# A decoder layer with routed experts: two products for the last 64 inner rows, the lower outputs added on VectorE, each tile's expert read ahead of the transposes

## The chip, the cores and the metric

The kernel runs on one core of one Trainium2 chip. The metric is the device time of an execution in microseconds. The kernel before took 1031.85 us (median of 3 runs, 1031.57 to 1033.68).

## The reference, cut to what matters

The layer is a state-space mixer, a cross attention and a routed feed-forward block, each added to x (2048 tokens of 256 numbers, fp32). The change lies in the last block:

```python
scores = xt @ Wg.T                                   # 2048 tokens, 8 experts
topk_scores, topk_idx = jax.lax.top_k(scores, 2)
gate = jax.nn.silu(jnp.einsum('td,ehd->teh', xt, W1))  # H = 704 inner rows
up = jnp.einsum('td,ehd->teh', xt, W2)
y = jnp.einsum('teh,edh->ted', gate * up, W3)
...
out = jnp.einsum('te,ted->td', w, y)                 # w: the two scores of a token
```

## The kernel before

Two phases follow each other: `mixer_phase` (everything up to the router's scores, to about 700 us) and `routed_ffn_phase`, the only one that the diff touches.

**Sorting.** VectorE and TensorE work out for each token its two positions in a list sorted by expert. Each expert's rows are padded to whole tiles of 128, so there are at most NT = 39 tiles, and all 39 are computed. With these inputs the list ends before the last ones. The table `tile_expert` holds each tile's expert. GpSimd gathers the 39 tiles of tokens (`tok`), and SP copies tile i + 4 to `tok_in` after it has stored the output of tile i (`store_and_load`).

**One tile.** TensorE transposes 128 tokens (ps_x). ScalarE rounds them to fp32r (`tokT_hi`) and VectorE keeps the rest (`tokT_lo`), and the weights are split in the same way (`w_hi`, `w_lo`). A product is then made as three: hi by hi, hi by lo, lo by hi. `gate_up` makes the gate and up products, 24 matmuls of 352 columns in two halves c = 0 and 1. ScalarE applies SiLU (`act_`) and VectorE multiplies by up (`multiply`, into `hid`). `transpose_hidden` transposes the 704 inner values in six pieces, five of 128 rows and the last of 64 (H_LAST). ScalarE (`round_hidden`) and VectorE (`rest_of_hidden`) split them. `down` makes 6 x 3 matmuls of 256 columns into ps_y, `evacuate` copies that to `y_sb`, and SP stores it to `ffn_sorted` in HBM.

**Order on TensorE.** The work is skewed by one tile: for tile i it is transpose_hidden(i-1), transpose_tokens(i+1), gate_up(i), down(i-1). Two tiles make one `pair`, which a hardware loop (`Fori`, L1581) repeats, and the last tiles are written out. `expert(i)` is a register load from `tile_expert` by PE's own sequencer (L1514); gate_up and down each make one, right ahead of their matmuls.

**Weights.** An expert's weights lie in one of two buffers. SP loads experts 0 to 3 and GpSimd experts 4 to 7 (`load_expert`, `reload`), with four DMAs each. The last, L1129, brings the 64 remaining rows of W3. The lower 64 partitions of that piece, in the weights and in hidT, are zero from a memset and two casts at the phase's start (`w_pad`), so all matmuls run over 128 rows. GpSimd splits the weights of experts 2 to 7, each as soon as the tiles of the expert two before are done (`next_expert`, `split`).

**The end.** Each token has a lower and an upper position. GpSimd gathers the lower outputs (`fetch` into `y_one`) when the tiles of experts 0 to 6 are stored (`stored(0)`). It waits for all sixteen, multiplies and adds the first eight groups of tokens into `x_all` (L1258, L1261), and then gathers the upper outputs (`y_two`, the space of `tok`) once all used tiles are stored (`stored(1)`). VectorE adds the other eight lower groups ahead of the last evacuation (L1481), combines all sixteen with the upper ones (L1491), and SP stores two groups at a time.

Of the kernel before, what the change touches and what calls it, by code (L numbers as in the profile page):

```python
# [5 lines left out]
F32 = mybir.dt.float32  # L6
# [14 lines left out]
def at(i, n=1):  # L21
    return bass.ds(i, n)
# [989 lines left out]
def routed_ffn_phase(nc, io, dims, env, sem, buf):  # L1012
# [12 lines left out]
    LOOP = NT + 2  # L1025

    with ExitStack() as ctx:
# [12 lines left out]
        hid = sb("hid", [P, 2, HF])  # L1040
# [62 lines left out]
        w_pad, hi_ok, w_ok = sem("w_pad"), sem("hi_ok"), sem("w_ok")  # L1103
# [14 lines left out]
        low_part, low_in, low_in2 = sem("low_part"), sem("low_in"), sem("low_in2")  # L1118
        BY_POOL = G // 2

        def load_expert(eng, e, p, done):

            w, full, last = w_raw[:, p, :], (KH - 1) * P, NW - D
            for n, src in enumerate((io["w1T"], io["w2T"])):
# [4 lines left out]
            eng.dma_start(w[0:H_LAST, last:NW], io["w3T"][at(e), full:HF, :].rearrange("a p d -> p (a d)")  # L1129
                          ).then_inc(done, 16)  # L1130
# [10 lines left out]
        with nc.Block() as block:  # L1141
# [42 lines left out]
            def _(pool):  # L1184
# [47 lines left out]
                for p in range(2):  # L1232
                    next_expert(2 + p, p, first_ld[p], 128)
                    reload(pool, 2 + p, p, wts_ld[p])
                with pool.Fori(2, E // 2 - 1) as j:
                    for p in range(2):
                        next_expert(2 * j + p, p, wts_ld[p], 64 * (j - 1))
                        reload(pool, 2 * j + p, p, wts_ld[p])
                for p in range(2):
                    next_expert(E - 2 + p, p, wts_ld[p], 64 * (E // 2 - 2))  # L1240
# [25 lines left out]
            def _(act):  # L1266
# [11 lines left out]
                def round_hidden(i):  # L1278
# [3 lines left out]
                    nc.scalar.copy(hidT_hi[:, 4:KH - 1, :], ps_h1[:, 0:(KH - 5) * P].rearrange("p (c m) -> p c m", m=P)  # L1282
                                   ).then_inc(hT_hi, 1)
                    nc.scalar.copy(hidT_hi[0:H_LAST, KH - 1, :], ps_h1[0:H_LAST, (KH - 5) * P:(KH - 4) * P]).then_inc(hT_hi, 1)

                act.wait_ge(w_pad, 1)
                for p in range(2):

                    act.wait_ge(first_ld[p], 64)
# [25 lines left out]
            def _(dve):  # L1315
# [118 lines left out]
                def rest_of_hidden(i):  # L1434
                    for k, (c, n, rows_in, bank) in enumerate(((0, 4, P, ps_h0), (4, KH - 5, P, ps_h1), (KH - 1, 1, H_LAST, ps_h1))):
                        dve.wait_ge(hT_hi, 3 * i + (1 if k == 0 else 3))
                        wait(dve, y_mm, i)
                        col = c % 4 * P if k < 2 else (KH - 5) * P
                        nc.vector.tensor_tensor(hidT_lo[0:rows_in, c:c + n, :],  # L1439
                                                bank[0:rows_in, col:col + n * P].rearrange("p (c m) -> p c m", m=P),  # L1440
                                                hidT_hi[0:rows_in, c:c + n, :].bitcast(F32), ALU.subtract).then_inc(hT_lo, 1)
# [25 lines left out]

                pair(1)
# [3 lines left out]
                rest_of_tokens(NT - 1, 0)  # L1472
                multiply(NT - 2, 1)
                evacuate(NT - 3, 0)
                rest_of_hidden(NT - 2)
                multiply(NT - 1, 0)
                evacuate(NT - 2, 1)
                rest_of_hidden(NT - 1)
                dve.wait_ge(low_ld, 16 * G)
                for g in range(BY_POOL, G):  # L1480
                    nc.vector.scalar_tensor_tensor(out=x_all[:, g, :], in0=y_one[:, g, :], scalar=w_low[:, 0, g:g + 1],  # L1481
                                                   in1=x_all[:, g, :], op0=ALU.mult, op1=ALU.add).then_inc(low_in2, 1)
                evacuate(NT - 1, 0)

                for g in range(G):
                    if g < BY_POOL:
                        dve.wait_ge(low_in, g + 1)
                    else:
                        dve.wait_ge(low_in2, g - BY_POOL + 1)
# [5 lines left out]
            def _(pe):  # L1495
# [33 lines left out]
                def gate_up(i, p):  # L1529
                    e = expert(i)  # L1530
# [13 lines left out]
                def transpose_hidden(i, p):  # L1544
# [5 lines left out]
                    for c in range(4, KH):  # L1550
                        n = P if c < KH - 1 else H_LAST
                        last = nc.tensor.transpose(ps_h1[0:n, (c - 4) * P:(c - 3) * P], hid[:, p, c * P:c * P + n], ident[:])  # L1552
                    last.then_inc(h_mm, 1)

                def down(i):
# [5 lines left out]
                    for c in range(KH):  # L1561
                        for n, (x, w) in enumerate(parts):
# [80 lines left out]
```

## Time and profile before

| | |
|---|---|
| median of 3 runs | 1031.85 us |
| profiled execution | 1034.26 us |
| its span, first to last instruction | 1032.4 us |
| mean granted TensorE clock | 0.916 |
| TensorE busy | 883.8 us (86%), 5148 matmuls |
| VectorE busy | 669.6 us (65%) |
| ScalarE busy | 447.0 us (43%) |
| GpSimd busy | 606.3 us (59%) |

Engines are PE (TensorE's matmuls), PEld (its weight loads), DVE (VectorE), ACT (ScalarE), POOL (GpSimd) and SP; a q behind the name is the engine's sequencer or DMA queue. L1563 is line 1563 of the kernel before. Times of instructions count from the span's start. Matmuls overlap in the array, so their starts tell more than their durations. In the chain of waits, "issue" is time in which an engine waited for nothing that the profile shows.

### The profile page before, as it was taken

How to read it: one execution, taken by the hardware profiler on the slowest of the kernel's cores; microseconds unless marked ns; L12 is line 12 of the kernel's file. 1: busy time of each engine (PE TensorE's matmuls, PEld its weight loads, DVE VectorE, ACT ScalarE, POOL GpSimd, SP SyncE). 2: the span in 40 equal slices, each digit the busy share in tenths (PEclk: the TensorE clock that was granted, in tenths of full speed). 3: DMA queues.
4: the chain of work that ended last, by engine and by line, in shares of the span. 5: the costliest groups of instructions: out<-in, count | busy, mean ns of one | idle time of the engine just before them, and what ended most of it. 6: DMA issues, size and time to landing. Idle time of an engine off the chain costs nothing. (4 is left out here: it accounts for less than half of the span.)

```text
span 1032.4 us, 16281 instructions
## 1 busy us (share of the span) xinstructions
PE 883.8 (86%) x5148; PEld 709.2 (69%) x5149; DVE 669.6 (65%) x1091; ACT 447.0 (43%) x827; POOL 606.3 (59%) x499
## 2 busy tenths in 40 slices
PE   5766776999998999988999778973699999999991
PEld 2334354667776676876588655763599999999991
DVE  4089789888799888798788943327643443444344
ACT  2544755446764547664456512223122333233230
POOL 2056787487766487766887613200778663355575
PEclk9979876999996999998999968995799999999996
DMA  9560013000044000063000400004464513311324
GB/s 313 185 234 1 0 43 122 2 16 1 2 183 145 1 17 1 2 220 107 9 10 1 140 25 16 1 21 168 155 215 105 172 45 115 120 41 36 101 66 154
DMA packets 48955, 85.45 MB, mean 83 GB/s; under 512 B 6292, under 2 KB 38696, under 8 KB 46856
## 3 DMA queue, kind: packets, MB, share of 16 engines
q1 hardware_dynamic: 43032, 65.77, 18.9%
q0 software_dynamic: 5872, 19.02, 6.2%
q8 instruction: 29, 0.48, 0.2%
q14 instruction: 22, 0.18, 0.1%
HBM read 65.64 MB, written 14.55 MB: 78 GB/s over the span
## 5 line engine op out<-in xcount | busy, mean ns | idle before, releaser
L417 POOL TENSOR_TENSOR u<-dtx,b_all 128x512 f32<-128x512 f32 x256 | 326.1, 1287 | 148.2 <-DVE h L666 140.8
L666 DVE TENSOR_TENSOR_SCAN h<-da,u 128x512 f32<-128x512 f32 x256 | 307.5, 1215 | 44.3 <-ACT da L501 27.1
L501 ACT ACTIVATE da<-dt_,a_neg 128x512 f32<-128x512 f32 x256 | 175.3, 691 | 119.5 <-DVE h L666 118.6
L789 PEld LDWEIGHTS ysum<-ident,h 128*128 128x128 f32 x1024 | 129.1, 152 | 68.3 <-issue 36.2
L789 PE MATMUL ysum<-ident,h 128*128 128x128 f32 x1024 | 150.2, 290 | 16.0 <-DVE h L666 11.1
L969 PE MATMUL pv<-pT,ctx_n 128*128 128x128 f32 (+1 forms) x832 | 103.6, 276 | 2.0 <-ACT pT L568 1.7
L969 PEld LDWEIGHTS pv<-pT,ctx_n 128*128 128x128 f32 (+1 forms) x832 | 98.1, 192 | 6.4 <-ACT pT L568 2.1
L940 PE MATMUL pa<-ctx_t,xnT_a 128*128 128x401 f32 (+1 forms) x256 | 93.7, 502 | 3.4 <-DVE sim L649 2.0
L1425 DVE TENSOR_TENSOR hid<-act_,ps_u 128x352 f32<-128x352 f32 x78 | 40.7, 521 | 84.0 <-ACT act_ L1276 84.0
L778 PE MATMUL pm<-xs,w_dt 128*128 128x512 f32 x128 | 71.5, 667 | 10.9 <-ACT sp_pos L537 4.7
L1276 ACT ACTIVATE act_<-ps_g 128x352 f32<-128x352 f32 x78 | 36.3, 465 | 102.2 <-PE ps_u L1539 102.2
L772 PE MATMUL pm<-xnT_m,w_in 128*128 128x512 f32 x128 | 68.7, 654 | 7.9 <-DVE xs L623 5.2
L940 PEld LDWEIGHTS pa<-ctx_t,xnT_a 128*128 128x128 f32 x256 | 45.3, 190 | 33.6 <-DVE sim L649 5.2
L1563 PE MATMUL ps_y<-w_hi,hidT_hi 128*128 x234 | 66.2, 283 | 2.1 <-DVE hidT_lo L1439 2.0
L1563 PE MATMUL ps_y<-w_hi,hidT_lo 128*128 x234 | 66.3, 283 | 0.0
L1563 PE MATMUL ps_y<-w_lo,hidT_hi 128*128 x234 | 66.1, 283 | 0.0
L1228 POOL DMA_INDIRECT tok<-xn_dram,tok_id x39 | 43.9, 1127 | 35.8 <-DVE tok_id L1407 24.2
L1281 ACT CAST hidT_hi<-ps_h 128x512 fp32r<-128x512 f32 x39 | 22.9, 587 | 90.9 <-PE ps_h L1552 90.9
L649 DVE COPY_PREDICATED sim<-mask,pa 128x401 f32<-128x401 uint8 x64 | 38.4, 601 | 34.8 <-PE pa L940 22.3
L1439 DVE TENSOR_TENSOR hidT_lo<-ps_h,hidT_hi 128x512 fp32r<-128x512 f32 (+2 forms) x117 | 42.0, 415 | 28.4 <-ACT hidT_hi L1281 28.4
L1202 POOL TENSOR_TENSOR w_lo<-w_raw,w_hi 128x2816 fp32r<-128x2816 f32 (+1 forms) x12 | 58.6, 4883 | 0.0
L440 POOL TENSOR_SCALAR sim<-mask,neg_c 128x1601 f32<-128x1601 uint8 x16 | 25.7, 1605 | 54.9 <-PE pa L955 27.5
(217 smaller groups left out, 1739.2 us busy)
## 6 DMA issues: line engine op xcount, KB each, us to landing
b_all<-b_dram SPq DMA_DIRECT2D x16, 1024.0 KB, 4.9
ctx_t<-in_ctxT SPq DMA_DIRECT2D x4, 1601.0 KB
ctx_n<-in_ctx SPq DMA_DIRECT2D x4, 1536.0 KB
ffn_sorted<-yg SPq DMA_DIRECT2D x1, 4992.0 KB, 22.5
ffn_sorted<-y_sb SPq DMA_DIRECT2D x39, 128.0 KB, 1.7
tok_in<-tok SPq DMA_DIRECT2D x35, 128.0 KB, 2.0
mask<-in_mask SPq DMA_DIRECT2D x16, 200.1 KB, 2.4
w_raw<-in_w1T SPq DMA_DIRECT2D x4, 704.0 KB, 4.4
```

The costliest lines, as they stand in the source:

```text
L417: nc.gpsimd.tensor_tensor(u[:, i % 2, :], dtx[:, j % 2, :], b_all[:, n, :], ALU.mult).then_inc(u_ok, 1)
L501: nc.scalar.activation(da[i % DS][:], dt_[:, j % 2, :], ACT.Exp, scale=a_neg[:, j, n:n + 1]).then_inc(da_ok, 1)
L666: nc.vector.tensor_tensor_scan(h[:, i % HS, :], da[i % DS][:], u[:, i % 2, :], 0.0, ALU.mult, ALU.add).then_inc(scan_ok, 1)
L772: last = nc.tensor.matmul(bank[:], w_in[:, k, j * P:(j + 1) * P], xnT_m[:, k, :], start=k == 0, stop=k == KD - 1)
L778: last = nc.tensor.matmul(DT_BANKS[j][:], w_dt[:, k, j * P:(j + 1) * P], of_row(xs, b, k), start=k == 0, stop=k == KI - 1)
L789: last = nc.tensor.matmul(ysum[:, t * P:(t + 1) * P], h[:, i % HS, t * P:(t + 1) * P], ident[:], is_transpose=True, start=n == 0 and t == ...
L940: last = nc.tensor.matmul(pa[c % 2][:, 0:hi - lo], xnT_a[:, k, q * P:(q + 1) * P], ctx_t[:, k, lo:hi], start=k == 0, stop=k == KD - 1)
L969: last = nc.tensor.matmul(pv[:, k * P:(k + 1) * P], ctx_n[0:w, c, k * P:(k + 1) * P], pT[0:w, c, :], start=c == 0 and k == 0, stop=c == KC ...
L1202: nc.gpsimd.tensor_tensor(w_lo[:, p * NW + lo:p * NW + hi], w_raw[:, p, lo:hi], w_hi[:, p * NW + lo:p * NW + hi].bitcast(F32), ALU.subtrac ...
L1228: pool.indirect_dma_start(tok[:, i, :], None, xn3_dram, bass.IndirectOffsetOnAxis(ap=tok_id[:, i:i + 1], axis=0)).then_inc(tok_ld[i // 2 % ...
L1439: nc.vector.tensor_tensor(hidT_lo[0:rows_in, c:c + n, :], bank[0:rows_in, col:col + n * P].rearrange("p (c m) -> p c m", m=P), hidT_hi[0:r ...
L1563: last = nc.tensor.matmul(ps_y[:, 0:D], x[:, c, :], w[:, at(e % 2 * NW + (2 * NGU + c * D), D)], start=c == 0 and n == 0, stop=c == KH - 1 ...
```

## The change

1. **Two products for the last piece.** `hid` is 768 columns wide. For c = 1, VectorE first writes the last 64 columns once more behind the 704. The sixth transpose then has 128 rows: the last 64 inner rows twice. ScalarE rounds all of it in one cast with the piece ahead of it (two casts in place of three), and VectorE replaces the lower copy by its remainder, in place: the piece holds hi on top and lo below. The last 64 rows of W3 are loaded twice, into both halves, by one more DMA per expert. `down` needs two products for this piece, by w_hi and by w_lo, so it has 17 matmuls. The memset and the casts of zeros are gone, and each expert counts five DMAs (WLD = 80).
2. **Lower outputs.** GpSimd no longer multiplies and adds: it goes from the gather of y_one to `stored(1)` and the gather of y_two. VectorE adds all sixteen lower groups (`add_lower`) in five lots of 3, 3, 3, 4 and 3, between its work for tiles 36 to 38.
3. **Expert.** In `pair` and in the last tiles, `expert(i)` for gate_up is read ahead of the transposes instead of behind them.

```diff
+    WLD = 16 * 5
-        hid = sb("hid", [P, 2, HF])
+        hid = sb("hid", [P, 2, KH * P])
...
             eng.dma_start(w[:, 2 * NGU:last].rearrange("p (c d) -> p c d", d=D), ...
-            eng.dma_start(w[0:H_LAST, last:NW], io["w3T"][at(e), full:HF, :].rearrange("a p d -> p (a d)")
-                          ).then_inc(done, 16)
+            for half in range(2):
+                eng.dma_start(w[half * H_LAST:(half + 1) * H_LAST, last:NW],
+                              io["w3T"][at(e), full:HF, :].rearrange("a p d -> p (a d)")).then_inc(done, 16)
...
                 stored(0)
                 fetch(y_one, 0, lambda g: low_ld)
-                pool.wait_ge(low_ld, 16 * G)
-                for g in range(BY_POOL):
-                    nc.gpsimd.tensor_scalar(y_one[:, g, :], y_one[:, g, :], w_low[:, 0, g:g + 1], None,
-                                            ALU.mult).then_inc(low_part, 1)
-                    pool.wait_ge(low_part, g + 1)
-                    nc.gpsimd.tensor_tensor(x_all[:, g, :], x_all[:, g, :], y_one[:, g, :], ALU.add).then_inc(low_in, 1)
                 stored(1)
                 fetch(y_two, 1, lambda g: up_ld[g // 2])
...
-                    nc.scalar.copy(hidT_hi[:, 4:KH - 1, :], ps_h1[:, 0:(KH - 5) * P].rearrange("p (c m) -> p c m", m=P)
+                    nc.scalar.copy(hidT_hi[:, 4:KH, :], ps_h1[:, 0:(KH - 4) * P].rearrange("p (c m) -> p c m", m=P)
                                    ).then_inc(hT_hi, 1)
-                    nc.scalar.copy(hidT_hi[0:H_LAST, KH - 1, :], ps_h1[0:H_LAST, (KH - 5) * P:(KH - 4) * P]).then_inc(hT_hi, 1)
-
-                act.wait_ge(w_pad, 1)
...
-                nc.vector.memset(w_raw[H_LAST:P, :, NW - D:NW], 0.0).then_inc(w_pad, 1)
-                dve.wait_ge(w_pad, 1)
-                for part in (hidT_hi, hidT_lo):
-                    nc.vector.tensor_copy(part[H_LAST:P, KH - 1, :], w_raw[H_LAST:P, 0, NW - D:NW - D + P]).then_inc(w_pad, 1)
...
+                        if c == 1:
+                            nc.vector.tensor_tensor(hid[:, p, HF:KH * P], act_[:, HF - H_LAST:HF],
+                                                    ps_u[c][:, HH - H_LAST:HH], ALU.mult)
                         nc.vector.tensor_tensor(hid[:, p, c * HH:(c + 1) * HH], ...
...
+                    low_half = hidT_hi[H_LAST:P, KH - 1, :]
+                    nc.vector.tensor_tensor(low_half, ps_h1[H_LAST:P, (KH - 5) * P:(KH - 4) * P], low_half.bitcast(F32),
+                                            ALU.subtract).then_inc(hT_lo, 1)
...
+                def add_lower(first, last):
+
+                    dve.wait_ge(low_ld, 16 * G)
+                    for g in range(first, last):
+                        nc.vector.scalar_tensor_tensor(out=x_all[:, g, :], in0=y_one[:, g, :], scalar=w_low[:, 0, g:g + 1],
+                                                       in1=x_all[:, g, :], op0=ALU.mult, op1=ALU.add).then_inc(low_in, 1)
...
                 rest_of_tokens(NT - 1, 0)
+                add_lower(0, 3)
                 multiply(NT - 2, 1)
                 evacuate(NT - 3, 0)
+                add_lower(3, 6)
                 rest_of_hidden(NT - 2)
+                add_lower(6, 9)
                 multiply(NT - 1, 0)
                 evacuate(NT - 2, 1)
+                add_lower(9, 13)
                 rest_of_hidden(NT - 1)
-                dve.wait_ge(low_ld, 16 * G)
-                for g in range(BY_POOL, G):
-                    nc.vector.scalar_tensor_tensor(...)
+                add_lower(13, G)
                 evacuate(NT - 1, 0)
...
                     for c in range(KH):
-                        for n, (x, w) in enumerate(parts):
+                        for n, (x, w) in enumerate(parts if c < KH - 1 else parts[0:2]):
...
                 def pair(i):
                     for k in range(2):
+                        e = expert(i + k)
                         transpose_hidden(i + k - 1, k)
                         transpose_tokens(i + k + 1, k)
-                        gate_up(i + k, 1 - k)
+                        gate_up(i + k, 1 - k, e)
                         down(i + k - 1)
```

## Rows read from the trace of the kernel before

**Rows 1.** busy time by stage: TensorE, its weight loads, VectorE, ScalarE, GpSimd, clock, DMA
```profile
720.00:740.00 20.00, 11.37 (x49) 10.13 (x49) 11.54 (x23) 1.79 (x5) 12.13 (x9) 0.58 0.38 127
780.00:820.00 40.00, 40.00 (x290) 39.85 (x290) 16.83 (x41) 12.11 (x36) 35.45 (x25) 1.00 0.46 135
```

**Rows 2.** chain of waits in order of time, one tile (start us, us, what)
```profile
834.93 0.96 PE ps_g L1539 x6
...
838.77 2.15 PE ps_y L1563 x18
841.79 1.03 PE ps_g L1539 x6
```

**Rows 3.** chain of waits, start-up, one stall, and the last gather
```profile
700.20 0.50 DVE w_raw L1331
...
741.65 0.60 issue
...
750.10 7.27 DMA tok_in<-tok
...
757.92 0.80 issue
758.72 1.22 PE ps_g L1539 x6
...
890.24 0.83 issue
...
1024.09 2.89 DMA tok<-ffn_sorted,pos
```

**Rows 4.** timeline of TensorE, first matmuls of tiles 31, 35, 38 and last down
```profile
953.32 0.42 PE L1539 MATMUL ps_g<-w_hi,tokT_hi 128*128 x1
...
981.06 0.42 PE L1539 MATMUL ps_g<-w_hi,tokT_hi 128*128 x1
...
1001.42 0.41 PE L1539 MATMUL ps_g<-w_hi,tokT_hi 128*128 x1
...
1010.36 0.38 PE L1563 MATMUL ps_y<-w_hi,hidT_hi 128*128 x1 [2.04 <-DVE hidT_lo L1439]
```

**Rows 5.** timeline of GpSimd, the two gathers and the work between
```profile
963.53 1.03 POOL L1243 DMA_INDIRECT y_one<-ffn_sorted,pos  x1 [0.52 <-issue]
...
982.40 0.95 POOL L1243 DMA_INDIRECT y_one<-ffn_sorted,pos  x1 [0.30 <-issue]
985.24 0.93 POOL L1258 TENSOR_SCALAR y_one<-y_one,w_low 128x256 f32<-128x256 f32 x1 [1.90 <-DMA y_one<-ffn_sorted,pos]
...
1000.69 1.03 POOL L1243 DMA_INDIRECT tok<-ffn_sorted,pos  x1 [0.54 <-issue]
...
1010.79 3.24 POOL L1243 DMA_INDIRECT tok<-ffn_sorted,pos  x1 [0.30 <-issue]
```

**Rows 6.** timeline of VectorE, one tile's product, and the end
```profile
839.30 0.52 DVE L1425 TENSOR_TENSOR hid<-act_,ps_u 128x352 f32<-128x352 f32 x1 [1.38 <-ACT act_ L1276]
...
1009.97 3.23 DVE L1481 SCALAR_TENSOR_TENSOR x_all<-y_one,w_low,x_all 128x256 f32<-128x256 f32 x8
...
1013.47 3.23 DVE L1491 SCALAR_TENSOR_TENSOR x_all<-tok,w_low,x_all 128x256 f32<-128x256 f32 x8
...
1027.07 0.88 DVE L1491 SCALAR_TENSOR_TENSOR x_all<-tok,w_low,x_all 128x256 f32<-128x256 f32 x2 [1.53 <-DMA tok<-ffn_sorted,pos]
```

**Rows 7.** PE's sequencer by line, ns and start, behind the loop's branch of tile 15
```profile
L1581 PEldq FUSED_REGOPS  x1: 59/59/59, 839.5 to 839.5; - x1
...
L1514 PEldq TENSOR_LOAD <-tile_expert x1: 300/300/300, 840.5 to 840.5; - x1
...
L1539 PEldq FUSED_REGOPS  x1: 104/104/104, 841.4 to 841.4; - x1
```

**Rows 8.** timeline of all engines where an expert's reload begins
```profile
883.45 0.76 POOL L1125 DMA_DIRECT2D w_raw<-in_w1T  x1 [0.30 <-POOL w_lo L1202]
...
883.66 0.49 SPq L1152 DMA_DIRECT2D tok_in<-tok  x1
```

More of the change, by code:

```diff
@@ L1232, in _ @@
                 for p in range(2):
-                    next_expert(2 + p, p, first_ld[p], 128)
+                    next_expert(2 + p, p, first_ld[p], 2 * WLD)
                     reload(pool, 2 + p, p, wts_ld[p])
@@ L1434, in rest_of_hidden @@
                 def rest_of_hidden(i):
[L1435 to L1441, printed above, removed]
+                    wait(dve, y_mm, i)
+                    dve.wait_ge(hT_hi, 2 * i + 1)
+                    for c, n, bank in ((0, 4, ps_h0), (4, KH - 5, ps_h1)):
+                        if c:
+                            dve.wait_ge(hT_hi, 2 * i + 2)
+                        nc.vector.tensor_tensor(hidT_lo[:, c:c + n, :], bank[:, 0:n * P].rearrange("p (c m) -> p c m", m=P),
+                                                hidT_hi[:, c:c + n, :].bitcast(F32), ALU.subtract).then_inc(hT_lo, 1)
+                    low_half = hidT_hi[H_LAST:P, KH - 1, :]
+                    nc.vector.tensor_tensor(low_half, ps_h1[H_LAST:P, (KH - 5) * P:(KH - 4) * P], low_half.bitcast(F32),
+                                            ALU.subtract).then_inc(hT_lo, 1)
                 def evacuate(i, p):
@@ L1472, in _ @@
                 rest_of_tokens(NT - 1, 0)
+                add_lower(0, 3)
                 multiply(NT - 2, 1)
                 evacuate(NT - 3, 0)
+                add_lower(3, 6)
                 rest_of_hidden(NT - 2)
+                add_lower(6, 9)
                 multiply(NT - 1, 0)
                 evacuate(NT - 2, 1)
+                add_lower(9, 13)
                 rest_of_hidden(NT - 1)
-                dve.wait_ge(low_ld, 16 * G)
-                for g in range(BY_POOL, G):
-                    nc.vector.scalar_tensor_tensor(out=x_all[:, g, :], in0=y_one[:, g, :], scalar=w_low[:, 0, g:g + 1],
-                                                   in1=x_all[:, g, :], op0=ALU.mult, op1=ALU.add).then_inc(low_in2, 1)
+                add_lower(13, G)
                 evacuate(NT - 1, 0)
                 for g in range(G):
[L1486 to L1489, printed above, removed]
+                    dve.wait_ge(low_in, g + 1)
                     dve.wait_ge(up_ld[g // 2], 32)
@@ L1527, in transpose_tokens, with gate_up @@
                     last.then_inc(x_mm, 1)
-                def gate_up(i, p):
-                    e = expert(i)
+                def gate_up(i, p, e):
                     pe.wait_ge(w_ok, 2 * e + 1)
@@ L1550, in transpose_hidden @@
                     for c in range(4, KH):
-                        n = P if c < KH - 1 else H_LAST
-                        last = nc.tensor.transpose(ps_h1[0:n, (c - 4) * P:(c - 3) * P], hid[:, p, c * P:c * P + n], ident[:])
+                        last = nc.tensor.transpose(ps_h1[:, (c - 4) * P:(c - 3) * P], hid[:, p, c * P:(c + 1) * P], ident[:])
                     last.then_inc(h_mm, 1)
@@ L1561, in down @@
                     for c in range(KH):
-                        for n, (x, w) in enumerate(parts):
+                        for n, (x, w) in enumerate(parts if c < KH - 1 else parts[0:2]):
                             last = nc.tensor.matmul(ps_y[:, 0:D], x[:, c, :],
                                                     w[:, at(e % 2 * NW + (2 * NGU + c * D), D)],
-                                                    start=c == 0 and n == 0, stop=c == KH - 1 and n == 2)
+                                                    start=c == 0 and n == 0, stop=c == KH - 1 and n == 1)
                     last.then_inc(y_mm, 1)
-                pe.wait_ge(w_pad, 3)
                 transpose_tokens(0, 0)
                 transpose_tokens(1, 1)
-                gate_up(0, 0)
+                gate_up(0, 0, expert(0))
                 def pair(i):
                     for k in range(2):
+                        e = expert(i + k)
                         transpose_hidden(i + k - 1, k)
                         transpose_tokens(i + k + 1, k)
-                        gate_up(i + k, 1 - k)
+                        gate_up(i + k, 1 - k, e)
                         down(i + k - 1)
@@ L1584, in _ @@
                 transpose_tokens(NT - 1, 0)
-                gate_up(NT - 2, 1)
+                gate_up(NT - 2, 1, expert(NT - 2))
                 down(NT - 3)
                 transpose_hidden(NT - 2, 1)
-                gate_up(NT - 1, 0)
+                gate_up(NT - 1, 0, expert(NT - 1))
                 down(NT - 2)
```

11 lines of the change are left out of this document (5 added, 6 removed).

## The prediction

> **What bounds the kernel now.** I read the table by stage first. From 780 to 820 us the matrix unit is busy 40.00 of 40 us at a granted clock of 1.00 [rows 1]: while the experts' tiles run, TensorE is the bound. The chain of waits gives one tile: its gate and up products start at 834.93, the 18 down products take 2.15 us, and the next tile starts at 841.79, 6.86 us later [rows 2]. One down product is therefore 2.15 / 18 = 0.12 us. Tile 3 starts at 758.72 [rows 3] and tile 38, the last, at 1001.42 [rows 4]: 242.70 us for 35 tiles, which is 2.6 us more than 35 x 6.86. Part of the 2.6 us is one stall of 0.83 us at 890.24 [rows 3]; the rest is small ones.
>
> After the tiles the bound changes. The chain that ended last doesn't leave through TensorE: it goes through GpSimd's queue [rows 5]. The first gather (y_one) starts at 963.53, the eight multiply-and-add pairs at 985.24, and the second gather (y_two) only at 1000.69. Its last issue is at 1024.09 and lands 2.89 us later [rows 3]; VectorE combines from 1027.07 for 0.88 us [rows 6], and the span ends at 1032.4, that is 4.45 us after the last combination. The last tile's first down product is at 1010.36 [rows 4], long before. So the tail is GpSimd's order of work: what brings the second gather forward is gained until VectorE takes over.
>
> When may the second gather start? It waits for the last used tile. The reference's inputs route 354, 538, 550, 585, 609, 596, 366 and 498 rows to the experts, which fill 3, 5, 5, 5, 5, 5, 3 and 4 tiles, 35 in all; tiles 35 to 38 are computed but never gathered. The first gather waits for tile 30, the second for tile 34.
>
> **The down products.** 39 tiles lose one product of 0.12 us each. The array-bound tile goes from 6.86 to 6.74 us. That only comes through if nothing else ends last. The hidden transposes wait for VectorE's product (0.52 us from 839.30 [rows 6]), then PE's sequencer issues eight transposes, loads the tile's expert at 840.5 and reaches the gate products at 841.4 [rows 7], while the array runs dry at about 841.5. On tiles behind the loop's branch (tile 15, 841.79) the sequencer is the later of the two by 0.07 us, which the chain shows as 1.03 instead of 0.96 for the first six products [rows 2]. With the shorter down and the load left in place, those tiles would gain nothing.
>
> **The expert's load moved ahead.** From the load to the gate products is 0.9 us, at most 0.75 of it the load's own [rows 7]. Ahead of the transposes it lies in the wait for the hidden product. Behind the branch (over at 839.6) the sequencer has 0.2 us until that product is there at 839.8, so transposes would be issued at 840.35 instead of 839.9. The array needs them at 840.92 less 0.12 [rows 2]: hidden, with some 0.4 us to spare. Bounds: nothing, or the whole 0.75 on 18 tiles if the array needed them sooner. I take hidden. Where the array stood idle the load is plainly on the path: 0.60 us at 741.65 and 0.80 at 757.92 [rows 3]. At 741.65 the next down product waits for VectorE's weight split, so I count nothing; at 757.92 I count 0.75.
>
> **Duplicated columns and rows.** VectorE's extra product covers 64 of the 352 columns that cost 0.52 [rows 6]; between 0.09 (in proportion) and 0.52, taken as 0.2. It delays the transposes' release, which has 0.8 us to spare before the array arrives. ScalarE's two casts in place of three, and VectorE's third subtraction on the upper 64 rows, are off the path. The second copy of the last 64 rows is one more DMA per expert, 64 KB, on SP for experts 0 to 3 and on GpSimd for 4 to 7. GpSimd has over 15 us between experts. On SP it lies ahead of the load of tile 4, which took 7.27 us behind weights [rows 3]. 64 KB more there is 0.1 to 0.6 us; I take 0.35. The memset at the start (0.50 us [rows 3]) and two casts of some 0.2 us go from VectorE's chain; it still needs GpSimd's counters, so I take 0.6 of the 0.9 (bounds 0 and 0.9).
>
> **Token loads against weight loads.** The 0.83 at 890.24 follows a token load that SP issued at 883.66, 0.21 us behind GpSimd's first weight load at 883.45 [rows 8]. GpSimd's split of an expert has a fixed length, two tiles get 0.24 us shorter or more, so the token load slips ahead of the weights. I count 0.5 us of stalls kept instead of 1.3.
>
> **The sum up to the last tile.** Tile 3: 0.6 (start) + 0.12 (down of tile 0) + 0.75 (expert) - 0.35 (DMA) = 1.1 us earlier. Tiles 3 to 38: 35 x 6.74 + 0.5 = 236.4 instead of 242.7, 6.3 less. Tile 38 starts at 994.0.
>
> **The tail.** Tile 31's start to the first gather, across tile 30's down and its store, is 963.53 - 953.32 = 10.21 us [rows 4, 5]. Tile 35 started at 981.06; it starts 1.1 + 5.8 = 6.9 earlier, so the second gather could start at 974.15 + 10.21 - 0.12 = 984.2. GpSimd is free by then, its pairs, which held it from 985.24 on, being gone and its first gather being over at about 977. That is 16.5 us earlier than 1000.69. Fifteen issues of the first gather took 982.40 - 963.53 = 18.87 us to the start of the sixteenth, 1.26 each [rows 5]; undisturbed, the last issue of the second starts at 1003.1 and ends at 1004.0.
>
> They are disturbed. The issue at 1010.79 took 3.24 us instead of 0.95, and ended at 1014.03, 0.83 after VectorE's eight additions (1009.97 + 3.23) [rows 5, 6]: an issue that starts while VectorE adds SBUF to SBUF waits for the run's end. The new kernel has five such runs, of 3, 3, 3, 4 and 3 additions at 0.404 us. Each holds up at most one issue, by 0 to 1.65 us; I take half, 2.9 in all. The last issue then starts near 1006.0 and ends at 1006.9, landing 1.9 us later.
>
> VectorE: y of tile 37 is copied out at about 1000.2, 0.4 us long, and four additions of 0.404 us follow; the subtraction on tile 38's hidden values, possible from 1001.3, comes behind them, 0.95 us late. Tile 38's down products start at 1010.36 - 7.4 - 0.12 + 0.95 = 1003.8, and the sixteen combinations at 1006.7, by the 3.1 us between the two before [rows 4, 6] less a product and a small overlap. They take 16 x 0.404 = 6.46 us and end at 1013.15, with all of y_two landed. Plus 4.45, plus 0.3 for eight output stores close together: a span of 1017.9, 14.5 less. The profiled execution took 1034.26 us, 1.86 more than its span, and the median of the runs is 1031.85; the difference goes to the median: 1017.3 us.
>
> The Trainium skill ("SBUF — State Buffer", two separate sides) calls the port pair of VectorE and GpSimd a lock held for a whole instruction, and lets a VectorE operation with two SBUF inputs take it only against a GpSimd operation that reads SBUF. By that condition an issue that only writes its descriptors would not be held up, and the last would end at 1004.0: the sum stays, since VectorE ends last in it, and the first rival below falls away. The row of 3.24 us speaks against it.
>
> **Rivals.** *The last gather is held up by the combinations* (0.24). If the five runs cost over 3.6 us instead of 2.9, GpSimd's last issue starts after 1006.7, when VectorE starts fourteen combinations in a row. These end at 1012.4, the issue 0.83 later, it lands after another 1.9, and two combinations end at 1016.0, 2.9 later than in the sum: 1020.2 us. For it: the two times lie within 0.7 us. Against it: runs of three end before most issues have waited long.
> *The tiles gain less* (0.13). Token loads behind the weights' extra 64 KB wait at each reload, or the sequencer still ends last behind the branch. The tiles then give 3 us instead of 6.3: 1020.6 us.
> *The stalls vanish altogether* (0.08): start and tiles give 1.5 more, 1015.8.
> *The change doesn't do what it says*: the pairs leave GpSimd, but the second gather is as late as before (0.02). That needs tile 37 or 38 among the used ones, which the rows per expert exclude. The gain would be the 7 us of the tiles: 1025.
> *Slower* (0.04): the granted clock. It was 0.58 from 720 to 740 and 1.00 afterwards [rows 1]; a tile at half clock costs 6.7 us more. If a moved wait near tile 4 let it fall, the sum turns from 14.5 / 6.7 = 2.2 such tiles on; with four, 1044. Of the chance, 0.01 is for about two such tiles and no change. Against it: that wait gets shorter, and before it stood at 1.00 through it.
>
> **How the numbers follow.** The forecast has 0.49, the rivals 0.24, 0.13, 0.08, 0.02 and 0.04. A measurement of this kernel tells 0.2% (2 us) from no change. Faster 0.96, within 0.2% 0.01, slower 0.03. The unknown terms (start 0 to 0.9, extra DMA 0.1 to 0.6, stalls 0 to 1.3, held-up issues 0 to 6.5) and the first three rivals give 1014.5 to 1022.5.
>
> **What would show it.** Right: 17 down products per tile, starts 6.74 apart on both kinds of tile; no issue time behind the token transposes near 757; the second gather's first issue near 984; VectorE's combinations as one run from 1006.7. Wrong: a steady tile above 6.8, idle TensorE ahead of the hidden transposes on every second tile, GpSimd issues of over 2 us between 990 and 1005, or a last issue that ends after a run of fourteen combinations.

## The result, and the profile after

The changed kernel takes 1018.16 us (median of 5 runs, 1017.06 to 1019.81) against 1033.60 for the kernel before (median of 5, the three of the prediction among them): a ratio of 0.9855 (95% interval 0.9833 to 0.9877). A later set of both gave 0.9829 (0.9787 to 0.9872). 1017.3 was forecast. The profiled execution took 1017.61 us, its span is 1015.8, its mean granted clock 0.921.

The total is right, but its last 0.9 us is luck: the span came out 2.1 us under the sum and the step from the span to the median 3.0 us over it. Two terms of the sum are wrong: held-up gather issues that don't occur, and an end that comes sooner than I added. The chain of waits shows start-up, one stall and one tile.

```profile
732.80 2.12 PE ps_g L1538 x6
...
749.22 8.18 DMA tok_in<-tok
...
757.53 0.43 PE ps_x L1526 x2
758.01 1.22 PE ps_g L1538 x6
...
799.06 6.35 DMA tok_in<-tok
...
806.04 1.22 PE ps_g L1538 x6
...
813.04 0.96 PE ps_g L1538 x6
...
816.86 2.04 PE ps_y L1561 x17
...
819.77 0.32 PE ps_g L1538 x2
```

Against [rows 2]: 17 down products in 2.04 us instead of 18 in 2.15, and the next gate products 6.73 us behind the last. 6.73 to 6.76 is the distance of all tiles from 4 to 37 but one, whether they follow the loop's branch or not; tile 38, ahead of which no tokens are left to transpose, comes 6.52 us behind tile 37 (6.64 before). Against [rows 3]: the issue time between the token transposes and tile 3's gate products (0.80) is gone, but the load ahead of it took 8.18 us instead of 7.27. A second late load (799.06) makes the one stall left: tile 10 starts 7.59 us behind tile 9.

The end, first TensorE (timeline, the first gate product and the first down product of tile 38), then GpSimd, then VectorE.

```profile
994.53 0.41 PE L1538 MATMUL ps_g<-w_hi,tokT_hi 128*128 x1
...
1004.13 0.38 PE L1561 MATMUL ps_y<-w_hi,hidT_hi 128*128 x1 [2.83 <-DVE hidT_hi L1435]
```
```profile
976.53 0.95 POOL L1244 DMA_INDIRECT y_one<-ffn_sorted,pos  x1 [0.30 <-issue]
983.01 0.20 POOL L1211 TENSOR_TENSOR pool_scrap<-ident 128x1 f32<-128x1 f32 x1 [5.52 <-DMA ffn_sorted<-y_sb]
...
984.35 0.98 POOL L1244 DMA_INDIRECT tok<-ffn_sorted,pos  x1 [0.52 <-issue]
...
1002.06 1.06 POOL L1244 DMA_INDIRECT tok<-ffn_sorted,pos  x1 [0.31 <-issue]
1003.43 0.95 POOL L1244 DMA_INDIRECT tok<-ffn_sorted,pos  x1 [0.30 <-issue]
```
```profile
1001.03 1.66 DVE L1467 SCALAR_TENSOR_TENSOR x_all<-y_one,w_low,x_all 128x256 f32<-128x256 f32 x4
1002.61 0.88 DVE L1432 TENSOR_TENSOR hidT_lo<-ps_h,hidT_hi 128x512 fp32r<-128x512 f32 x2
...
1003.85 1.28 DVE L1467 SCALAR_TENSOR_TENSOR x_all<-y_one,w_low,x_all 128x256 f32<-128x256 f32 x3
1006.46 0.42 DVE L1441 COPY y_sb<-ps_y 128x256 f32<-128x256 f32 x1 [1.34 <-PE ps_y L1561]
1006.80 6.41 DVE L1491 SCALAR_TENSOR_TENSOR x_all<-tok,w_low,x_all 128x256 f32<-128x256 f32 x16
```

GpSimd is idle 5.52 us until tile 34 is stored, and the second gather begins at 984.35, not at 1000.69 [rows 5]. Its sixteen issues are 1.27 us apart on the mean; the last ends at 1004.38, 2.4 us before VectorE is ready to combine. The sixteen combinations run through from 1006.80 to 1013.21, and the span ends 2.6 us later.

What ends the span can be read on the line that closes the program: each engine has a DRAIN there, and the program is over when the last of them is. First the kernel before, then the changed one (ns, and start in us):

```profile
L1141 POOLq DRAIN  x1: 24336/24336/24336, 1007.9 to 1007.9; - x1
...
L1141 SPq DRAIN  x1: 7/7/7, 1030.3 to 1030.3; - x1
```
```profile
L1142 POOLq DRAIN  x1: 19997/19997/19997, 991.9 to 991.9; - x1
...
L1142 SPq DRAIN  x1: 7/7/7, 1015.6 to 1015.6; - x1
```

In the kernel before, SP, which waits for the output stores, is done at 1030.3 and GpSimd only at 1007.9 + 24.3 = 1032.2: GpSimd ends the span. In the changed kernel GpSimd is done at 1011.9 and SP at 1015.6: the output stores end it.

The 16.6 us between the two spans divide so. Tile 0 starts at 732.80 instead of 733.90: 1.1. Tiles 0 to 3 take 25.21 instead of 24.82: -0.4. Tiles 3 to 38 take 236.52 instead of 242.70: 6.2. From tile 38's start to the end, 21.3 instead of 31.0: 9.7. These are distances in one profile of each kernel, and the start-up and the stalls differ from profile to profile by some 2 us.

### The profile page after: what moved, and what is told of

The parts are those of the page before. It is cut to its first block and busy times, and to the rows that moved or that the text cites. A ratio compares the mean times of both kernels' runs of the same rounds, so it can differ in the third digit from the quotient of the medians.

```text
span 1015.8 us, 16089 instructions
## 1 busy us (share of the span) xinstructions
PE 876.1 (86%) x5109; PEld 703.4 (69%) x5110; DVE 684.3 (67%) x1135; ACT 445.5 (44%) x788; POOL 592.2 (58%) x487
## 5 line engine op out<-in xcount | busy, mean ns | idle before, releaser
L1229 POOL DMA_INDIRECT tok<-xn_dram,tok_id x39 | 44.6, 1143 | 35.3 <-DVE tok_id L1396 23.7
L1561 PE MATMUL ps_y<-w_hi,hidT_lo 128*128 x195 | 55.3, 284 | 0.0
L1538 PE MATMUL ps_g<-w_hi,tokT_hi 128*128 x156 | 53.8, 345 | 0.7 <-issue 0.6
L1432 DVE TENSOR_TENSOR hidT_lo<-ps_h,hidT_hi 128x512 fp32r<-128x512 f32 x78 | 34.6, 486 | 28.3 <-ACT hidT_hi L1276 28.3
```

The lines of the kernel that those rows point to most:

```text
L1229: pool.indirect_dma_start(tok[:, i, :], None, xn3_dram, bass.IndirectOffsetOnAxis(ap=tok_id[:, i:i + 1], axis=0)).then_inc(tok_ld[i // 2 % ...
L1538: last = nc.tensor.matmul(out[:, 0:HH], x[:, p, k * P:(k + 1) * P], w[:, at(e % 2 * NW + (first + k * HF), HH)], start=k == 0 and n == 0, ...
L1561: last = nc.tensor.matmul(ps_y[:, 0:D], x[:, c, :], w[:, at(e % 2 * NW + (2 * NGU + c * D), D)], start=c == 0 and n == 0, stop=c == KH - 1 ...
```

## Experiments

Ratios are to the kernel before on the same chip. Distances are between first gate products (the first matmul of each tile); "35 tiles" is tile 3 to tile 38. A lot is one call of `add_lower`.

**The third product put back** for the last piece, all else changed.

```diff
-  for n, (x, w) in enumerate(parts if c < KH - 1 else parts[0:2]):
+  for n, (x, w) in enumerate(parts if c < KH - 1 else parts[0:2] + parts[0:1]):
```


> The changed kernel with a third matmul for the last piece again (the first of its two products is made once more, so the last 64 inner rows count too much in the output). If the array bounds the tiles, as forecast, each of 35 steady tiles goes from 6.74 back to 6.86 us, and the span from 1015.8 to about 1020.3 (39 x 0.12). Rival: something beside the array ends last in a tile (sequencer, VectorE), then the product is free: tiles stay at 6.74 and the span within 0.5 of 1015.8.

Measured: 1022.16 us, 0.9894 (0.9866 to 0.9922). The tile is 6.86 us again, with 2.15 us for x18 in the chain of waits:

```profile
864.74 2.15 PE ps_y L1561 x18
...
867.77 0.96 PE ps_g L1538 x6
```
35 tiles take 239.93 us, which is 34 x 6.86 and 6.64 for tile 38, without a stall. So the product is worth its 0.12 us on each tile, 4.0 us in the medians. The stall at tile 10 is absent. It goes with the time at which the token load that it waits for is issued, counted from the first of GpSimd's weight loads: 2.35 us behind it in the changed kernel's second profile (stall 1.9), 3.8 in its first (0.85), 4.15 in the kernel before with the expert ahead (0.2), 4.6 here and 5.0 in the kernel before (none). A longer tile puts the load further behind the weight loads.

**The expert read behind the transposes**, as before.

```diff
-                        e = expert(i + k)
                         transpose_hidden(i + k - 1, k)
                         transpose_tokens(i + k + 1, k)
+                        e = expert(i + k)
```


> The changed kernel with each tile's expert read behind the transposes, as before; all else stays. Forecast theory: the sequencer is released by VectorE's product, which now ends 0.14 us later, and then needs transposes, load and gate products in a row: the tiles behind the loop's branch take about 7.0 us and the others about 6.9 instead of 6.74, the span is 5 to 8 us longer (1021 to 1024). Rival 1: only the tiles behind the branch lose, 0.1 to 0.2 us each: 2 to 3 us. Rival 2: the load is hidden wherever it stands: under 0.5 us.

Measured: 1027.10 us, 0.9942 (0.9920 to 0.9964); 35 tiles take 244.33 us, more than the 242.70 of the kernel before. The tiles alternate between 7.06 and 6.89. The chain of waits, a tile behind the branch and the one after it, and VectorE in one of them:

```profile
909.54 0.44 PE ps_h L1547 x4
...
910.42 0.06 issue
910.48 1.22 PE ps_g L1538 x6
...
914.56 2.04 PE ps_y L1561 x17
...
917.47 1.12 PE ps_g L1538 x6
```
```profile
901.15 0.22 DVE L1415 TENSOR_TENSOR hid<-act_,ps_u 128x64 f32<-128x64 f32 x1 [1.30 <-ACT act_ L1271]
901.29 0.51 DVE L1417 TENSOR_TENSOR hid<-act_,ps_u 128x352 f32<-128x352 f32 x1
```
The first group of gate products takes 1.22 or 1.12 us where it needs 0.96: the array has run dry and waits for its sequencer. This is a loop that doesn't pass through the down products: gate and up products, SiLU, VectorE's product, the transposes' release, the expert's load, the next gate products. VectorE's new 64-column product sits in it and puts off the 352-column one by 0.14 us (901.15 to 901.29).

The starts of matmuls on TensorE's timeline show the loop's two parts. Here it is tiles 23, 24 and 25:

```profile
896.53 0.42 PE L1538 MATMUL ps_g<-w_hi,tokT_hi 128*128 x1
...
903.42 0.42 PE L1538 MATMUL ps_g<-w_hi,tokT_hi 128*128 x1
...
910.48 0.42 PE L1538 MATMUL ps_g<-w_hi,tokT_hi 128*128 x1
```
From a tile's first gate product to the end of VectorE's 352-column product (901.29 + 0.51) it is 5.27 us, against 5.13 in the kernel before (834.69 to 839.82): 0.14 more. From there to the next tile's first gate product it is 1.62 us, and 1.78 or 1.79 when that tile is behind the branch (1.78 in the kernel before, 839.82 to 841.60). The sums, 6.89 and 7.06, are the two distances; so the sequencer's part is fixed, and VectorE's 0.14 us goes into every tile. Without the 64-column product the same parts would give 6.91 behind the branch and 6.75 elsewhere; that is worked out, no run has it. I had forecast no gain for the tiles behind the branch with the load left in place; they lose 0.1 us, and the other tiles gain nothing. In the medians the load's place is worth 8.9 us.

**The expert ahead alone**, in the kernel before.

```diff
+                        e = expert(i + k)
                         transpose_hidden(i + k - 1, k)
                         transpose_tokens(i + k + 1, k)
-                        gate_up(i + k, 1 - k)
+                        gate_up(i + k, 1 - k, e)
...
```


> The kernel before with nothing changed but each tile's expert read ahead of the transposes. Forecast theory: tiles behind the loop's branch lose their 0.05 to 0.1 us of waiting for the sequencer, so all steady tiles take 6.86 to 6.87, and the idle 0.80 us near 757.9 goes: tile 3 starts 0.7 earlier and the tiles take 1 us less, but the end is GpSimd's, whose first gather moves by 1.5: the span gets 0.7 to 2 us shorter. Rival: behind the branch the load now ends last and those tiles get longer (over 6.96), the span is the same or longer.

Measured: 1029.98 us, 0.9979 (0.9961 to 0.9998). All tiles are 6.86 us (one stall, 7.08), 35 of them 240.13, which is 2.6 less than in the kernel before, where 1 was expected. 1.1 of the 2.6 is the kernel before's stall ahead of tile 22 (7.96), which its second profile doesn't have there; the other 1.5 is the up to 0.1 us by which most tiles lay above 6.86. So by itself the move is worth about 1.5 us of the tiles; together with the shorter down it decides whether that one counts at all.

**GpSimd's eight pairs put back**, VectorE's eight additions in one lot.

```diff
                 fetch(y_one, 0, lambda g: low_ld)
+                pool.wait_ge(low_ld, 16 * G)
+                for g in range(BY_POOL):
+                    nc.gpsimd.tensor_scalar(y_one[:, g, :], ...)
+                    nc.gpsimd.tensor_tensor(x_all[:, g, :], ...)
                 stored(1)
...
-                add_lower(0, 3) ... add_lower(9, 13)
-                add_lower(13, G)
+                add_lower(BY_POOL, G)
```


> The changed kernel with GpSimd's eight multiply-and-add pairs between the gathers again and VectorE's other eight additions in one lot ahead of the last evacuation. Forecast theory: the second gather starts at about 994.5 instead of 984.35, its last issue ends between 1014.4 and 1017, and the span is 1021 to 1024. Rival: the end is VectorE's anyway, because its combinations can't start before 1006; then the span stays below 1018.

Measured: 1024.61 us, 0.9926 (0.9901 to 0.9952). The second gather starts at 992.88; from tile 38 to the end it is 28.1 us instead of 21.3, so the pairs are worth 6.8 us (6.5 in the medians). Its last issue ends at 1013.4, GpSimd's DRAIN at 1020.9 and SP's at 1019.4, the span at 1021.1: it is GpSimd's end again. GpSimd's timeline beside VectorE's:

```profile
992.88 1.04 POOL L1245 DMA_INDIRECT tok<-ffn_sorted,pos  x1 [0.54 <-issue]
...
1004.25 1.23 POOL L1245 DMA_INDIRECT tok<-ffn_sorted,pos  x1 [0.30 <-issue]
...
1008.27 1.21 POOL L1245 DMA_INDIRECT tok<-ffn_sorted,pos  x1 [0.30 <-issue]
```
```profile
1001.79 3.26 DVE L1474 SCALAR_TENSOR_TENSOR x_all<-y_one,w_low,x_all 128x256 f32<-128x256 f32 x8
...
1005.42 4.04 DVE L1497 SCALAR_TENSOR_TENSOR x_all<-tok,w_low,x_all 128x256 f32<-128x256 f32 x10
```
Five issues start within these two runs, and the longest is 1.23 us. An issue that meets such a run is not always held up.

**No second copy of the last rows** for experts 2 to 7.

```diff
-            for half in range(2):
+            for half in range(halves):      # halves = 1 for experts 2 to 7
```


> The changed kernel without the second copy of the last 64 rows of W3 for experts 2 to 7 (the upper half keeps the rows of expert 0 or 1, so the output is another). If that DMA is what makes the token load of tile 4 land 0.9 us later (8.18 instead of 7.27) and the one of tile 12 stall TensorE for 0.85 us, both get shorter: tile 3 starts 0.5 to 0.9 earlier, the stall is below 0.5, the span 1 to 1.7 shorter (1014.1 to 1014.8). Rival: the stall comes from when the token load is issued relative to the weights, not from 64 KB more; then it stays within 0.2 us.

Measured: 1016.09 us, 0.9833 (0.9804 to 0.9861). Tile 3 starts 8.73 us behind tile 2 (9.37 in the changed kernel, 7.83 in its second profile, below), and the stall at tile 10 (the expectations count it as tile 12) is 7.63, as in the changed kernel. The 64 KB don't make the stall; their cost at tile 3 is lost in what that load varies by between profiles, and the interval of the ratio overlaps those of the changed kernel (0.9855 and 0.9829).

**All sixteen additions in one lot**, behind the last hidden remainder; and **two lots of eight**.

```diff
-                add_lower(0, 3) ... add_lower(9, 13)
+                add_lower(0, G)      # one lot: in place of add_lower(13, G)
+                add_lower(0, 8) ... add_lower(8, G)      # two: ahead of both rest_of_hidden
```


> The changed kernel with all sixteen lower additions in one lot between the subtraction on tile 38's hidden values and the last evacuation. The lot runs from about 1002.7 for 6.4 us, so the evacuation and the combinations start some 2.7 us later (1009.5). Theory of the forecast (an issue that starts during a run of VectorE additions waits for the run's end): the two or three gather issues that are left then wait up to 5 us, the last ends near 1012 and lands at 1014: span 1019 to 1022. Rival (only operations or runs of a certain kind hold it up, as no issue was held up in the changed kernel): issues stay at 0.96 us and the span is 1018 to 1019, set by VectorE's order alone.

> The changed kernel with the lower additions in two lots of eight (3.2 us each), behind the evacuation of tile 36 and of tile 37. Theory that long runs hold up GpSimd's gather issues: one issue in each lot takes 2 to 3.3 us instead of 0.96, and the last ends 2 to 5 us later (1006.5 to 1009.5 instead of 1004.4). Rival: all issues stay at 0.96 us, because what held up the two issues before lay elsewhere. Both: tile 38's down products come 1.5 to 3 us later than 1004.1, since the lots delay tile 37's and tile 38's subtractions, and the span is 1017 to 1020.

Measured: 1019.92 us, 0.9881 (0.9846 to 0.9916), and 1019.61, 0.9874 (0.9838 to 0.9909). In one lot only the last gather issue was left; it began 0.02 us ahead of the additions and took 0.95 us, so this run hardly tests the theory. The additions lie on the path ahead of the last evacuation, and the combinations start at 1009.07. In two lots, the last issue inside each took 1.22 and 1.25 us and the last of all ended at 1003.67, so the theory fails here. The second lot holds back tile 38's remainders, and then something else comes up (chain of waits):

```profile
1000.84 0.23 PE ps_h L1547 x2
...
1002.36 1.67 DVE x_all L1467 x4
...
1005.47 4.00 PE ps_y L1558 x17
```
The seventeen down products, which need 2.3 us, take 4.00. The table by stage shows the granted clock as 0.50 there (1.2 of 2.4 GHz), behind 4.4 us in which TensorE did nothing and within which it had begun to fall (0.90):

```profile
1001.07:1005.47 4.40, 0.00 (x0) 0.01 (x1) 4.05 (x11) 0.86 (x2) 2.21 (x2) 0.90 0.42 120
1005.47:1007.87 2.40, 2.40 (x11) 2.40 (x12) 0.00 (x0) 0.00 (x0) 0.00 (x0) 0.50 0.00 0
```

**Tiles 4 and 5 transposed straight from the token tile**, to take away the load ahead of tile 3; and again, with the changed kernel, on one chip.

```diff
+        DIRECT = 6
-                    load(i + AHEAD, (q + AHEAD) % GROUP)
+                    if not (isinstance(i, int) and i + AHEAD < DIRECT):
+                        load(i + AHEAD, (q + AHEAD) % GROUP)
...
-                    if isinstance(i, int) and i < AHEAD:
+                    if isinstance(i, int) and i < DIRECT:
```


> The changed kernel with one more pair of tiles written out on TensorE, and tiles 4 and 5 transposed straight from the gathered tokens, so that no copy of them queues behind the weights of expert 3. Theory: the 1.5 us for which tile 3 waits for that copy go, tile 5 starts 1 to 1.6 us earlier and so does all that follows, span 1014.3 to 1015.0. Rival: the wait turns up again at the first tile that is copied (tile 6), or a later copy meets weights that come as early as before, and the span stays within 0.5 us of 1015.8.

> The changed kernel, unchanged, beside the one with tiles 4 and 5 transposed straight from the tokens, on one chip: 1018 us within 1.5, the wait ahead of tile 3 (9.4 us between the first gate products of tiles 2 and 3, where a steady tile has 6.74) and one stall near tile 12 (7.6 us) again. No gather issue longer than 1.3 us from 984 us on, if the held-up issues don't belong to this kernel; one or more of 2 us and over if it is chance.

> Tiles 4 and 5 transposed straight from the token tile, as before, timed beside the changed kernel on one chip. If the wait ahead of tile 3 is really removed, the time is 1.0 to 2.6 us less than the changed kernel's (9.37 less 6.74 at most); if it only moves to the next loads, which then wait in the same queue, less than 1 us. From tile 0 to tile 38 the trace should then need 1 to 2.6 us less, or the same.

Measured: 1015.90 us (0.9852, 0.9821 to 0.9883) at first; on one chip 1016.76 (0.9831, 0.9788 to 0.9873) beside 1016.96 for the changed kernel: no difference. In the second profile the wait at tile 3 is gone (6.73), but tile 8 now starts 7.66 behind tile 7, and tile 10 8.42 behind tile 9. Its chain of waits:

```profile
782.72 6.22 POOL w_lo L1207
...
789.22 1.22 PE ps_g L1542 x6
...
796.31 7.48 DMA tok_in<-tok
```
From tile 0 to tile 38 it needs 260.9 us and the changed kernel's second profile 261.3. Without the wait at tile 3 the tiles reach the next expert's weights sooner and wait for their split (6.22) and for the token load behind their DMAs. The wait is moved, not removed. In the changed kernel's second profile the distances of tiles 3 and 10 were 7.83 and 8.65 where the first had 9.37 and 7.59: 16.5 and 17.0 in sum. No gather issue in it took over 1.1 us.

**The kernel before, profiled a second time.** 

> The kernel before, unchanged, profiled a second time: do GpSimd's two held-up gather issues (3.24 and 3.19 us, in the profile of before) come again? If VectorE's run of eight 128x256 additions holds an issue up as a matter of course, both come back at about 3.2 us. If it is a matter of when in the run the issue starts, or of chance, they take 0.95 to 1.25 us as in the changed kernels, and the last issue ends some 2 to 4 us sooner after the run before it. In both cases the steady tile is 6.86 us, and the time is within 2.5 us of 1033 us.

Measured: 1033.22 us. GpSimd and VectorE:

```profile
1010.19 0.95 POOL L1243 DMA_INDIRECT tok<-ffn_sorted,pos  x1 [0.30 <-issue]
1011.45 3.20 POOL L1243 DMA_INDIRECT tok<-ffn_sorted,pos  x1 [0.30 <-issue]
1014.95 0.95 POOL L1243 DMA_INDIRECT tok<-ffn_sorted,pos  x1 [0.30 <-issue]
```
```profile
1010.58 3.24 DVE L1481 SCALAR_TENSOR_TENSOR x_all<-y_one,w_low,x_all 128x256 f32<-128x256 f32 x8
...
1014.87 4.10 DVE L1491 SCALAR_TENSOR_TENSOR x_all<-tok,w_low,x_all 128x256 f32<-128x256 f32 x10
```
The first held-up issue comes again (it ends at 1014.65, 0.83 us after the run), the second doesn't, though it meets a longer run. The kernel with the expert ahead alone had both (3.02 and 3.19). 35 tiles took 245.12 us here, against 242.70: its stalls (the longest distance is 9.29, ahead of tile 12) differ between its two profiles by more than the changed kernel's.

**One gather more, after the eighth combination**, in the changed kernel.

```diff
+                sp.wait_ge(low_ld, 16 * (G + 1))
                 sp.wait_ge(out_st, 16 * (G // 2))
...
                 fetch(y_two, 1, lambda g: up_ld[g // 2])
+                pool.wait_ge(comb, 8)
+                pool.indirect_dma_start(y_one[:, 0, :], None, ffn_sorted, ...pos[:, 0, 0:1]...).then_inc(low_ld, 16)
```


> The changed kernel with one gather more (into y_one's first group, which is no longer read), issued by GpSimd after VectorE's eighth combination. In three profiles of kernels that have the old tail (the kernel before, its second look, and the one with the expert ahead only) the span ends 8.3 to 8.4 us after the start of GpSimd's last gather issue, although the last combination is over 4 to 5 us earlier; in the changed kernel it ends 12.4 us after it and 2.6 us after the last combination. Theory: GpSimd's part of the program ends a fixed 8.3 us after its last gather issue, whatever else there is, and the kernel before was ended by that. Then the extra issue, which starts about 3.5 us after the first combination, moves the end to 8.3 us after itself, some 2.6 us later than in the changed kernel: about 11.7 us from the first combination to the end of the span instead of 9.0, and 1020.5 us. Rival: the end is that of the last output store, and an unread gather that lands before it costs nothing: 9.0 us from the first combination to the end, and about 1018 us.

Measured: 1024.07 us, 0.9916 (0.9886 to 0.9946), 5.9 us more than the changed kernel. GpSimd, VectorE and the line that closes the program:

```profile
1012.92 3.73 POOL L1261 DMA_INDIRECT y_one<-ffn_sorted,pos  x1 [6.45 <-DVE x_all L1495]
```
```profile
1009.41 6.41 DVE L1495 SCALAR_TENSOR_TENSOR x_all<-tok,w_low,x_all 128x256 f32<-128x256 f32 x16
```
```profile
L1142 POOLq DRAIN  x1: 11540/11540/11540, 1012.7 to 1012.7; - x1
...
L1142 SPq DRAIN  x1: 7/7/7, 1019.2 to 1019.2; - x1
```
The span is 1024.5 us. The last output store was issued by 1016.3, as early behind the combinations as in the changed kernel, yet the end is 8.7 us after the last combination. In this run SP also waits for the extra gather to land, but SP is done at 1019.2 and GpSimd at 1012.7 + 11.5 = 1024.2, so that wait isn't what ends it. Of the 8.7 us between the two spans 2.6 lie ahead of the combinations, most of them ahead of tile 38, and 6.1 behind. The theory is right in its mechanism and low in its size: the issue was itself held up, until 0.83 us after VectorE's run, and the span ends 7.8 us after the issue's end, which is 11.6 and not 8.3 after its start. In the kernel before, in its second profile and with the expert alone the end came 7.4 us after the last issue's end.

## Why the prediction was right, and where it was not

**The down products**: right. 6.74 was forecast for the tile and measured, and 236.4 us for tiles 3 to 38 became 236.52. Putting the third product back gives 6.86. But 6.86 was not what the kernel before needed. I took it from two pieces of the chain of waits; from first matmul to first matmul (834.69 to 841.60) that tile took 6.91. More than half of the 2.6 us that I put down to stalls was such hundredths on most tiles, and they went with the expert's load.

**The expert's load**: right, and the whole of the tiles' gain hangs on it: left behind the transposes, 35 tiles take 244.33 us. Hidden behind the branch, as taken; the 0.80 at tile 3 is gone. What I had not priced is that VectorE's extra product (0.14 us) lies in the same loop as the load. "It delays the transposes' release, which has 0.8 us to spare" holds only with the load moved; without, every tile is longer for it, as the two parts of the loop show.

**Token loads against weight loads**: 0.5 us of stalls forecast; one of 0.85 measured, of 1.9 in the second profile, none with the third product in. The row at 890.24 was one draw of something that differs from profile to profile; to take half of it was no better than a guess. That 236.4 and 236.52 lie so close is luck in part: 0.35 us more of stall, and 0.22 less for tile 38, which I had counted as a full tile.

**Tile 3**: 1.1 us earlier forecast, 0.7 measured, and for other reasons. Tile 0 came 1.1 earlier, of which about 0.65 had been gained before the phase that the diff touches (the scores are copied at 698.91 instead of 699.56, so it is no effect of the change), and from tile 0 to tile 3 0.4 us were lost where I had 0.5 gained. The second profiles (24.4 us before, 23.7 after) have the sign that I forecast. The late load eats or gives back the difference, so the 0.75 and the 0.35 can't be told apart there, and both stay open.

**The second gather**: right. 984.2 forecast for its first issue, 984.35 measured, by the store of tile 34 and not by GpSimd. With the pairs back it is 992.88 and the end 6.8 us later.

**Held-up issues**: wrong, 2.9 us forecast and 0.2 measured. "An issue that starts while VectorE adds SBUF to SBUF waits for the run's end" made a rule of two rows. Four profiles show six held-up issues, all ending about 0.83 us after the run; but twelve others started within runs of eight or ten and took 0.94 to 1.27 us, in kernels of either tail, and none that started within the shorter runs took over 1.14. Five of the six had started 0.82 to 1.04 us into a run of eight, and none of the twelve between 0.4 and 1.2 us; the sixth, the extra gather, started 3.5 us into sixteen. No run here varies that, so what decides it stays open. The forecast got by because 2.9 us of delay would have ended at 1006.9, when VectorE was only just ready: the term wasn't on the path, as the sum itself had it. The rival built on it (a last gather held up by the combinations) did not occur, and the lots of eight, meant to bring it about, didn't either. The condition in the Trainium skill ("SBUF — State Buffer", two separate sides), by which the last issue would have ended at 1004.0, comes nearer to the 1004.4 measured; but by that condition the six held-up issues, the 3.73 us of the extra gather among them, should not exist.

**VectorE's part**: right. Down products of tile 38 at 1004.13 (1003.8), combinations from 1006.80 (1006.7) to 1013.21 (1013.15). Tile 38 started 0.5 us later than forecast and this part was 0.5 us shorter.

**The end**: the term that failed on the path. I added the 4.45 us between the last combination and the end in the kernel before, and 0.3 for stores; it was 2.6. The 4.45 was no store time: it was GpSimd's, whose DRAIN ends 7.2 us after its last issue has ended, and the span 0.2 us later. In the kernel before, that is 1025.04 + 7.4 = 1032.4, its span, where SP with the stores was done 1.9 us earlier. In the changed kernel GpSimd is done at 1011.9, so the last output store decides. The extra gather shows it from the other side. So the gain of the tail is 9.7 us instead of 7.1, and the span came out 2.1 under the sum. The median lies 0.9 over the forecast all the same, because I had carried over from the kernel before that the median lies 2.4 us under the profiled execution; here it lies 0.5 over it. The two misses, 2.1 under and 3.0 over, have nothing to do with each other, and that they cancel is luck.

The clock (the slower rival) stayed at 1.00 in every stage of the tiles read, from 740 to 994 us.

## What to carry to other kernels

A time between the last useful instruction and the end of the span belongs to one engine's queue: find which one, on the line that closes the program, before carrying it over to a kernel whose order has changed. A sequencer's register load is cheap or dear by its place: list the loop that it closes (here SiLU, VectorE's product, release, load, next products), and price every other edit in that same loop before counting a shorter array time. And a late load that is issued behind bulk loads gives its wait to the next one when it is taken away.

## What the runs showed of the hardware

- **The end of a GpSimd queue with gathers.** In all fourteen profiles GpSimd's DRAIN ended 7.2 to 7.6 us after the end of its last indirect issue (1025.03 to 1032.2 in the kernel before, 1004.38 to 1011.9 in the changed one), even where the outputs were stored by then. Where it was the last engine, the span ended 0.2 us later: 7.4 us after the issue in three, with the pairs put back 7.7 and with the extra gather 7.8. With the last issue over 11 us before the end it played no part.
- **The clock in the last tile.** TensorE waits 2.83 us for tile 38's last remainder. In the changed kernel the granted clock stays 1.00 through the down products behind it (2.31 us); with the extra gather, and with the third product (3.03 us for 18), the same wait was followed by 0.81 and 0.83 in the table by stage. In the 4.4 us ahead TensorE was busy for 1.58 us in all three, at 1.00, so no row here tells them apart. With two lots of eight the wait was 4.41 us, the clock 0.50 and the products 4.00 us.
- **Held-up issues.** An issue into a run of VectorE's additions was held till 0.83 us after it, or by some 0.3 us at most, with the same operations on both engines. Two issues of the start-up were held by VectorE's weight split in the same way in the kernel before (4.88 us from 728.11 and 3.48 from 740.79).
